# The weighted expert sums of two layers, moved from a GpSimd tree to accumulating VectorE instructions

## What is computed

```python
def _L0_ffn_ref(x, Wr, br, W1, b1, g1, be1, m1, v1, W2, b2, g2, be2, m2, v2, Wo, bo):
    feat = jnp.mean(x, axis=0)
    w = jax.nn.softmax(feat @ Wr + br, axis=-1)
    ...
    y = jnp.einsum('bfeh,ehd->bfed', h, Wo) + bo
    return jnp.einsum('bfed,fe->bfd', y, w)

def _L1_ffn_ref(x, gate_w, gate_b, W1, b1, W2, b2):
    ...
    top2_vals, top2_idx = jax.lax.top_k(probs, 2)
    cw = jnp.zeros((N, Ee), dtype=xf.dtype).at[jnp.arange(N)[:, None], top2_idx].add(top2_vals)
    def step(acc, params):
        w1, bb1, w2, bb2, we = params
        h = jax.nn.gelu(xf @ w1 + bb1, approximate=False)
        y = h @ w2 + bb2
        return (acc + we[:, None] * y, None)
```

```python
        i_t = jax.nn.sigmoid(xi_t + h @ V_i)
        ...
        c_new = h * c + i_t * g_t
        h_new = o_t * jnp.tanh(c_new)
```

## Time and profile before

| | |
|---|---|
| median of 3 runs | 3875.54 us (3870.01 to 3875.71) |
| the profiled execution | 3875.58 us, of which the span is 3873.8 us |
| LSTM turns (32) | 267.5 to about 3117 us |
| start of the conv, attention and last expert phases | about 3120 us |
| PE busy | 2736.5 us (71%) |
| DVE busy | 2465.1 us (64%) |
| ACT busy | 1845.1 us (48%) |
| POOL busy | 809.9 us (21%) |

### The profile page before, as it was taken

How to read it: one execution, slowest core, us unless ns; L and a number is a source line. 1 busy time by engine, 2 the same in 40 slices (tenths; PEclk the granted TensorE clock), 3 DMA queues, 4 the chain that set the end, 5 groups by cost and what they waited for, 6 DMA issues and landing times. The chain is left out here.

```text
span 3873.8 us, 61926 instructions
## 1 busy us (share of the span) xinstructions
PE 2736.5 (71%) x15756; PEld 2072.8 (54%) x15756; DVE 2465.1 (64%) x10107; ACT 1845.1 (48%) x6798; POOL 809.9 (21%) x1419
## 2 busy tenths in 40 slices
PE   4677777776677776667777776777765379788766
PEld 2565555555555555555555555555554234455655
DVE  4766666666666666666666666666544477455778
ACT  1345555555555555555555555555544410444322
POOL 2332222222222222222222222222220000000010
PEclk9776666777666666666666777667655589999777
DMA  2000000000000000000000000000000010000000
GB/s 85 10 27 14 15 16 15 16 15 16 16 17 17 17 15 24 18 16 16 15 16 15 16 15 16 15 16 15 15 14 8 1 24 0 1 1 1 6 7 8
DMA packets 53969, 59.37 MB, mean 15 GB/s; under 512 B 26449, under 2 KB 45009, under 8 KB 53201
## 3 DMA queue, kind: packets, MB, share of 16 engines
q1 hardware_dynamic: 53584, 54.98, 4.6%
HBM read 42.35 MB, written 4.19 MB: 12 GB/s over the span
## 5 line engine op out<-in xcount | busy, mean ns | idle before, releaser
L1038 PE MATMUL psL<-r_h,lvab 128*96 128x16 f32 x2048 | 444.5, 296 | 752.0 <-DVE r_h L1067 703.6
L1038 PEld LDWEIGHTS psL<-r_h,lvab 128*96 128x96 f32 x2048 | 370.2, 230 | 971.8 <-DVE r_h L1067 905.3
L1047 ACT ACTIVATE r_wk<-psL 64x16 f32<-64x16 f32 x1024 | 188.5, 184 | 891.9 <-PE psL L1038 890.0
L1061 DVE TENSOR_TENSOR_SCAN r_c<-r_wk 64x24 f32<-64x24 f32 x1024 | 263.4, 257 | 532.8 <-ACT r_wk L1047 523.4
L1067 DVE SCALAR_TENSOR_TENSOR r_h<-r_wk,r_tc 64x8 f32<-64x8 f32 x2048 | 362.0, 177 | 359.8 <-ACT r_tc L1052 341.2
L1049 ACT ACTIVATE r_wk<-psL 32x8 f32<-32x8 f32 x2048 | 356.0, 174 | 37.4
L1052 ACT ACTIVATE r_tc<-r_c 64x8 f32<-64x8 f32 x1024 | 214.3, 209 | 268.8 <-DVE r_c L1061 256.4
L585 POOL TENSOR_TENSOR a_xw<-a_S,a_dtm 128x512 f32<-128x512 f32 x128 | 157.3, 1248 | 314.1 <-DVE a_dtm L511 314.1
L1070 DVE SCALAR_TENSOR_TENSOR r_wk<-r_h,r_c 64x8 f32<-64x8 f32 x1024 | 195.7, 191 | 35.6
L927 PE MATMUL psC<-m_xT,W 128*128 128x256 f32 x512 | 190.6, 484 | 1.0 <-ACT m_h L956 1.0
L385 PE MATMUL psA<-a_xw,a_RM 128*32 128x64 f32 x2048 | 184.2, 263 | 6.4 <-DVE state L544 6.4
...
## 6 DMA issues: line engine op xcount, KB each, us to landing
...
a_xy<-a_E SPq DMA_DIRECT2D x512, 16.0 KB, 1.8
...
```

The costliest lines, as they stand in the source:

```text
L1038: nc.tensor.matmul(psL[0:RM, par, c:c + 2 * LB], lvab[:], h, start=False, stop=False, skip_group_check=True).then_inc(sem("r_z"), 1)
L1047: nc.scalar.activation(o, psL[0:64, par, c:c + 2 * LB].rearrange("p (g b) -> p g b", b=LB), ACT.Tanh).then_inc(sem("r_gi"), 1)
L1061: v.tensor_tensor_scan(r_c3[:, t % 2, :], r_wk[:, 0:24], r_wk[:, 30:54], 0.0, ALU.mult, ALU.add).then_inc(sem("r_c"), 1)
```

## The change

Both expert sums move to DVE. A new helper `expert_sum` issues, for each expert e and each half j, one instruction that reads the expert's 64 channels from PSUM, multiplies them by the token's weight (a per-partition pointer), and adds X[:, i, j], in place: 16 instructions of 128 x 64 for each layer and tile. The two halves are independent of one another; expert e+1 waits by semaphore for expert e, for both halves. The last raises x2_done or x4_done. The buffer `f_big`, the four products and the tree on POOL go. Expert 0 is due at the first number of `acc`, experts 1 and 2 half a slot later, 3 and 4 at one slot later, and so on up to expert 7 at two slots later.

```diff
-    "f": dict(... y=(8.5, 11, 12, 12.5), big=(12.5, 14), tree=14.5),
+    "f": dict(... y=(8.5, 11, 12, 12.5), acc=(14, 14.5, 15, 15.5)),
-    "m": dict(... y=(12.5, 13.5, 14, 15), big=(14.5, 16), tree=16.5),
+    "m": dict(... y=(12.5, 13.5, 14, 15), acc=(16, 16.5, 17, 17.5)),
...
-        f_big = sb("f_big", P, J, E, C);
...
-            for j in range(J):
-                yield at["big"][j]
-                if j == 0:
-                    dve.wait_ge(sem("f_w"), i1)
-                dve.wait_ge(sem("f_y"), 2 * i + (j + 1))
-                v.tensor_tensor(f_big[:, j], psB[:, j].rearrange("p (e c) -> p e c", e=E), bc(f_w[:, 2], 2, C), ALU.mult)\
-                    .then_inc(sem("f_big"), 1)
+            yield at["acc"][0]
+            dve.wait_ge(sem("f_w"), i1)
+            dve.wait_ge(sem("f_y"), 2 * i + 2)
+            yield from expert_sum(dve, i, "f", psB, lambda j, e: f_w[:, 2, e:e + 1], at["acc"], "x2_done")
...
-        def experts_pool(pool, i, k, big, s0, done):
-            g = nc.gpsimd
-            yield s0
-            pool.wait_ge(sem(k + "_big"), 2 * i + 2)
-            st = Steps(pool, sem(k + "_halves"), i, 3)
-            for n in (4, 2, 1):
-                st.did(g.tensor_tensor(big[:, :, 0:n], big[:, :, 0:n], big[:, :, n:2 * n], ALU.add)); st.wait()
+        def expert_sum(dve, i, k, ps, weight, slots, done):
+            st = Steps(dve, sem(k + "_acc"), i, J * E - 1)
+            for e in range(E):
+                yield slots[e // 2] + e % 2 * 0.5
+                st.wait() if e else settle(dve)
+                for j in range(J):
+                    acc = nc.vector.scalar_tensor_tensor(X[:, i, j], ps[:, j, e * C:(e + 1) * C], weight(j, e), X[:, i, j], ALU.mult, ALU.add)
+                    if e == E - 1 and j == J - 1:
+                        acc.then_inc(sem(done), 1)
+                    else:
+                        st.did(acc)
             st.end()
-            settle(pool)
-            g.tensor_tensor(X[:, i], X[:, i], big[:, :, 0], ALU.add).then_inc(sem(done), 1)
...
-            for j in range(J):
-                yield at["big"][j]
-                dve.wait_ge(sem("m0_y"), 2 * i + (j + 1))
-                v.tensor_tensor(u["big"][:, j], psC[:, j].rearrange("p (e c) -> p e c", e=E), bc(u["cw"][:, j], 2, C), ALU.mult)\
-                    .then_inc(sem("m0_big"), 1)
+            yield at["acc"][0]
+            dve.wait_ge(sem("m0_cw"), i1)
+            dve.wait_ge(sem("m0_y"), 2 * i + 2)
+            yield from expert_sum(dve, i, "m0", psC, lambda j, e: u["cw"][:, j, e:e + 1], at["acc"], "x4_done")
```

More of the change, by code:

```diff
@@ L81 @@
     "a1": dict(ev=0, x=1, u=3, S=2.5, ser=3, R=4, bc=5, z=3, xw=5, bct=4.5, bcts=5, Tz=5.5, Sz=6, seg=7, E=7, sum=9, ex=10, sd=10.5, de=9.5, Gd=10.5, off=11.5, M=11, yo=12.5, state=13, Y=(14, 15.5), Yv=16.5, yd=16.5, y1=15, y2=20, ss=20, r2=20.5, yT=20.5, yTs=21.5, out=22.5, x1=24),
-    "f": dict(ln=0, rs=0, xn=0, xT=0.5, xTs=1, feat=1.5, lg=2.5, d=2.5, e=3.5, w=4.5, mm1=(2.5, 2.5, 3.5, 4), h=(3.5, 5, 6.5, 8), mm2=(5, 5.5, 8, 7), y=(8.5, 11, 12, 12.5), big=(12.5, 14), tree=14.5),
+    "f": dict(ln=0, rs=0, xn=0, xT=0.5, xTs=1, feat=1.5, lg=2.5, d=2.5, e=3.5, w=4.5, mm1=(2.5, 2.5, 3.5, 4), h=(3.5, 5, 6.5, 8), mm2=(5, 5.5, 8, 7), y=(8.5, 11, 12, 12.5), acc=(14, 14.5, 15, 15.5)),
     "c0": dict(ln=16, rs=16, xn=17, e=18, et=20, ets=21, mm=(21.5, 20.5, 23, 23.5), q=24.5, qT=27, l=28, x=29),
-    "m": dict(ln=1, rs=1, xn=2, xT=3, xTs=4, lg=5, d=7, p=7.5, top=(8.5, 9.5, 10), mm1=(5, 8.5, 8.5, 9, 10, 10.5, 11.5, 11.5), h=(8.5, 9.5, 11.5, 12.5), y=(12.5, 13.5, 14, 15), big=(14.5, 16), tree=16.5),
+    "m": dict(ln=1, rs=1, xn=2, xT=3, xTs=4, lg=5, d=7, p=7.5, top=(8.5, 9.5, 10), mm1=(5, 8.5, 8.5, 9, 10, 10.5, 11.5, 11.5), h=(8.5, 9.5, 11.5, 12.5), y=(12.5, 13.5, 14, 15), acc=(16, 16.5, 17, 17.5)),
     "c1": dict(ln=18.5, rs=18.5, xn=19.5, e=20.5, et=22, ets=22, mm=(23.5, 24, 24.5, 25), q=26, qT=27, l=28, x=29),
@@ L967, in mix_dve @@
             dve.wait_ge(sem("m0_lg"), i1)
-            st = Steps(dve, sem("m0_steps"), i, 8)
+            st = Steps(dve, sem("m0_steps"), i, 7)
             lg = psC[:, 1, 0:J * E].rearrange("p (j e) -> p j e", j=J)
@@ L988, in mix_dve @@
             st.did(last); st.wait()
-            st.did(v.tensor_tensor(u["cw"][:], p_, u["rest"][:, :, 0:E], ALU.subtract)); st.wait()
-            for j in range(J):
-                yield at["big"][j]
-                dve.wait_ge(sem("m0_y"), 2 * i + (j + 1))
-                v.tensor_tensor(u["big"][:, j], psC[:, j].rearrange("p (e c) -> p e c", e=E), bc(u["cw"][:, j], 2, C), ALU.mult)\
-                    .then_inc(sem("m0_big"), 1)
+            v.tensor_tensor(u["cw"][:], p_, u["rest"][:, :, 0:E], ALU.subtract).then_inc(sem("m0_cw"), 1)
             st.end()
+            yield at["acc"][0]
+            dve.wait_ge(sem("m0_cw"), i1)
+            dve.wait_ge(sem("m0_y"), 2 * i + 2)
+            yield from expert_sum(dve, i, "m0", psC, lambda j, e: u["cw"][:, j, e:e + 1], at["acc"], "x4_done")
         def xproj_pe(pe, i, mixed, par):
@@ L1202, in _ @@
                 ("mix", lambda n: ln_at(SLOT["m"]["rs"], "m0", mix1["ln"], 1e-5, n)),
-                ("mix", lambda n: experts_pool(pool, n, "m0", mix1["big"], SLOT["m"]["tree"], "x4_done")),
                 ("mix", lambda n: ln_at(SLOT["c1"]["rs"], "c1", c_ln[1], 1e-6, n)),
                 ("ffn", lambda n: ln_at(SLOT["f"]["rs"], "f", f_ln, 1e-5, n)),
-                ("ffn", lambda n: experts_pool(pool, n, "f", f_big, SLOT["f"]["tree"], "x2_done")),
                 ("ffn", lambda n: ln_at(SLOT["c0"]["rs"], "c0", c_ln[0], 1e-6, n)),
```

## The result

The changed kernel takes 3916.24 us (median of 4, 3915.58 to 3921.52), the kernel before beside it 3872.94 us (3870.01 to 3875.71): a ratio of 1.0115, 95% interval 1.0097 to 1.0132, slower by 43 us where 46.5 us were forecast. The profiled execution took 3915.58 us.

A forecast was written before the change was run, and what follows sets the result against it. DVE's own queue on the LSTM's thread was taken as the bound, with sums added and tree hold-ups removed netting +1.57 us a turn. Over 29 turns +45.5, plus 1: 3875.6 + 46.5 = 3922.1 us, range 3868 to 3965.

The forecast's parts named there:

- The stretch: DVE from the scan of step 15 to h times c of step 18: 10.62 or 11.20 us before, 12.48 after.
- The price of a sum: Each new DVE instruction 0.28 us, 0.20 start to start; two dependent pairs, experts such as 1 and 2, cost 0.91.
- The hold-ups: POOL's tree delays DVE reading SBUF on both sides or normalising; removing it takes about 3.0 us from a turn.
- 29 times +1.57: 29 turns with both layers beside the LSTM, each longer by a mean 1.57 us in the stretch: +45.5 us.
- clock stays up: Rival: without hold-ups PE's clock holds through slots 18 to 24, net -1.4 us a turn, 3835 us; chance 0.07.
- The prologue and the start: Turns before the LSTM: DVE sums of 4.1 us replace product, tree and last addition, about the same: 0.
- The free semaphore: Rival: dependent pairs follow like independent ones, 0.11 us less at six places a turn, -19 us, 3903; chance 0.05.
- Short sums: Rival: a 64-wide pair takes only 0.34 us, blocks 0.65, a turn ends at -0.25, 3868 us; chance 0.10.
- the dear semaphore: Rival: a dependent instruction's gap is 0.15 us, six times 0.12 more, +0.7 a turn, 3943 us; chance 0.10.
- The other rule: DVE with two SBUF inputs blocks fully beside POOL reading SBUF; at h of step 17 some 0.1 us a turn, 3 us.
- Slot 18: Expert 7 of m (0.48 us) is hidden behind PE's 16 matmuls; without that cover 0.40 us, +12 us in all.
- The clock that drops earlier: Rival: longer PE gaps make short turns long, +4.1 us each, for half the turns +60 us, 3982; chance 0.08.

The follow-up runs named there:

- no_tree: Kernel before without both layers' trees and last additions, products kept, expert outputs not added to X: 3784.84 us, 0.9769.
- f_alone: Only layer 0's (f's) sum on DVE as in the change, layer 1's (m's) as before with product and tree: 3905.23 us, 1.0078.
- idle_tree: Changed kernel with trees of the old shapes put back on POOL at their old slots, on buffers nothing else reads: 4000.57 us, 1.0326.
- Written out: The loop's 26 turns written out without jumps, in the kernel before (3840.22 us, 0.9928) and in the changed kernel (3869.24 us, 0.9992).
- split_waits: Changed kernel, but where two experts directly follow one another, each half waits only for the same half before it: 3914.12 us, 1.0106.

## Why the prediction was right, and where it was not

**What bounds the kernel.** Right. The stretch went from 10.91 to 12.25 us, and what the experiments took from it or added to it moved the time in step as long as the code and the clock stood still: no_tree -3.03 us and -88 us, f_alone +1.09 us and +33 us, 29 to 30 us of time for each us.

**The price of a sum.** Confirmed: 275 ns in the rows against 0.28. Blocks of two experts cost 0.87 to 0.90 us from start to start (1167.44 to 1168.31, 1163.71 to 1164.61) against 0.91. By the timeline of that turn, slot 14.5 took 1.38 us (forecast 1.40), slot 15 2.35 (2.39), slot 15.5 1.68 (1.72), slot 16.5 1.37 (1.39), slots 17 and 17.5 3.35 (3.38). The step that was mis-sized is slot 16, from h times c to the scan: 2.11 us at 1169.00 to 1171.11, forecast 2.20. I had put 0.15 us on the semaphore increment ahead of expert 0 of m, and 0.07 us stand there (1169.00 + 0.17 to 1169.24). The sum was 12.48, the stretch is 12.25.

**The hold-ups.** Right in kind (idle_tree) and in size (no_tree, 3.0 us on the mean of both kinds of turns, 2.8 in those of the earlier trace rows). Outside the stretch I had them too small: DVE's busy time was forecast at 2570 and is 2488. I had counted each sum with its full 0.28 us, where busy time counts overlap once (240 us for 1024 of them, not 283), and hold-ups of 90 us, where 2465.1 + 239.6 - 86.0 - 2488.4 leaves 130.

**29 times +1.57.** Here the forecast was right for a reason that is only half its own. The stretch gave +1.33 us (+1.63 and +1.04 in the two kinds of turns, forecast +1.86 and +1.28). I took the 11.20 us of the earlier trace rows as they stood and did not ask why they differ from 10.62: the late scan and the h times c behind the tree, 0.6 us in every second turn, which the changed kernel does not have. Written out, where that is gone from before as well, the stretch is +1.47. The rest of the turn was set at nothing. It has +0.98 us for late code and -0.95 us from the clock. The first I had not seen at all: each count of instructions on the page stood there (10107, and 896 more to come), and the mark "issue" stands ahead of f_st in before's rows with 2.1 us, and I asked only what the new instructions last, not what their code does to the loop. The second is the rival "clock stays up" in a small form: not in slots 18 to 24, where I looked for it, but above all in step 4 (-0.87 us); step 12 gave 0.37 and step 9 took the same 0.37 back. That the one term cancels the other is luck. Had the clock been as in split_waits, whose clock steps are those of before, the change would have cost some 28 us more by the table (29 x 0.95), and 3922 would have been too low.

**The prologue and the start.** Forecast at nothing. The first scan stands at 274.0 us, before at 267.5. So of the 40.0 us between the two profiled executions' spans only 34.5 lie between the first and the last scan, where the forecast had put all of its 46.5. Of the 6.5 us 4.3 are there before the first sum (at 136.88): the matmul of L641 that starts at 129.44 in before starts at 133.78. From 0 to 72 us the granted clock is 0.82 instead of 1.00. Some 2 us may be the sums in three turns without LSTM. In split_waits, with the same sums, the first scan stands at 267.9, so this is not shown to be the change's.

**The rivals.** The free semaphore is out: split_waits took 0.135 us for each of six waits. The Trainium skill, "VectorE: DVE Perf Modes", section "The DRAIN you can't avoid", has a chain with a semaphore after each instruction as long as one without; here the wait for the instruction directly ahead makes a block longer, 0.95 to 0.99 us against 0.83. Short sums are out (275 ns), the dear semaphore too (a dependent expert costs 0.135 us, not 0.23). The other rule weighed ahead of the result, on a DVE instruction with two SBUF operands beside POOL (the Trainium skill, "SBUF — State Buffer", section "Who interferes with whom"), holds for the tree (1.01 us for h in idle_tree); the overlap of h with the small L298 that would have cost 0.1 us does not occur in the changed turn shown, so its 3 us stay open. Slot 18 kept its cover: the matmul of step 20 starts 2.71 us after that of step 19 (1175.85 to 1178.56), as in the earlier trace rows. The clock that drops earlier did not come.

**The jump** has a rule too. The Trainium skill, "Runtime: NRT & Kernel Launch", section "Instruction fetch mechanics", says that a taken branch to code outside the present blocks makes the engine wait until a DMA has brought it. The traces agree: 3.9 to 4.3 us from the scan of step 31 to the next behind a jump, 1.75 without, and the long late starts only behind it. The small ones (0.17 us at the scan of step 17 in before, 0.3 to 0.4 in steps 14 and 20 of the changed kernel) stand in the loop's first iteration too, which is entered without a jump, and are nearly all gone written out; for them the rule is not enough. That the long ones appear with some 28 DVE instructions a turn more and not with 14 no page and no run explains beyond the one transfer more per iteration.
